# Two transformer layers on one core: heads' outputs with v as the weight, combine weights made in the small experts' loop, queries and values from split operands

## The reference

```python
h = layernorm(tok_w[x] + pos_w + type_w[mask]) * gamma + beta            # (32, 128, 192)
xn = layernorm(h)
h += softmax(causal(xn @ Wq @ Wk.T @ xn.T)) @ (xn @ Wv)                  # one head of 192
x = layernorm(h); logits = x @ phi_n.T                                   # 1024 slots = 64 experts x 16
slots = softmax(logits, over tokens).T @ x                               # dispatch
ys = gelu(layernorm(slots) @ w1[n] + b1[n]) @ w2[n] + b2[n]              # 64 small experts, hidden 384
h += softmax(logits, over slots) @ ys                                    # combine
q, k, v = split(layernorm(h) @ w_qkv.T); q, k = rope(q), rope(k)         # 12 heads of 16
h += softmax(q @ k.T) @ v @ w_proj.T + b_proj                            # no mask
x = layernorm(h); e = argmax(softmax(x @ router_w))                      # 8 experts, 512 rows each
h += gate * gelu(gelu(x @ w1[e] + b1[e]) @ w2[e] + b2[e])                # hidden 768
```

## Time and profile before

| what | value |
|---|---|
| time, median of 3 runs | 1556.29 us (1554.89 to 1559.04) |
| the profiled execution | 1558.22 us, its span 1556.5 us |
| tower, until PE's last slot sums | to about 382 us |
| small experts | to about 929 us |
| combine | to about 1402 us |
| large experts | to the end |
| busy share of the span | PE 92%, PEld 82%, DVE 63%, ACT 57%, POOL 17% |
| mean granted clock of TensorE | 0.934 |

### The profile page before, as it was taken

The page is one execution under the profiler, slowest core; times in us unless marked ns, Lnnn a source line. Parts: engine busy times, 40 slices in busy tenths (PEclk is TensorE's granted clock), DMA queues, the critical chain, the costliest instruction groups (busy, mean ns, idle before and its releaser), DMA issues. The chain is left out here.

```text
span 1556.5 us, 28510 instructions
## 1 busy us (share of the span) xinstructions
PE 1431.4 (92%) x8824; PEld 1269.1 (82%) x8824; DVE 978.6 (63%) x2877; ACT 891.0 (57%) x1833; POOL 270.8 (17%) x255
## 2 busy tenths in 40 slices
PE   3899999985899999999999986999999999957995
PEld 1577777774799999999999976999999999956985
DVE  6776666442777777777777744777776777632231
ACT  1377777774666666666666642655555555524551
POOL 5411100000111111111111101122121212120434
PEclk9999999998899999999999997889898989867998
DMA  7035655576466666666666654434333436105542
GB/s 198 25 123 146 146 135 135 140 172 149 136 200 186 193 189 196 187 190 197 189 189 190 199 155 148 129 108 126 114 125 99 121 116 190 31 11 148 134 91 20
DMA packets 202698, 220.87 MB, mean 142 GB/s; under 512 B 30065, under 2 KB 169528, under 8 KB 202606
## 3 DMA queue, kind: packets, MB, share of 16 engines
q1 hardware_dynamic: 170254, 179.96, 41.5%
q10 hardware_dynamic: 24672, 32.79, 6.2%
q0 software_dynamic: 7680, 6.95, 2.4%
HBM read 142.27 MB, written 79.90 MB: 143 GB/s over the span
## 5 line engine op out<-in xcount | busy, mean ns | idle before, releaser
L1062 PE MATMUL bank<-e_w,e_h_full 128*128 128x192 f32 x1920 | 324.5, 326 | 0.3
L1062 PEld LDWEIGHTS bank<-e_w,e_h_full 128*128 128x128 f32 x1920 | 310.6, 190 | 1.2 <-ACT e_h_full L1123 0.8
L1123 ACT ACTIVATE e_h_full<-bank,e_b 128x512 f32<-128x512 f32 x240 | 165.1, 689 | 196.7 <-PE bank L60 196.7
L1000 POOL TENSOR_TENSOR e_ln_rstd<-e_ln_var_eps,minus_half 128x4 f32<-128x4 f32 x64 | 64.8, 1013 | 524.2 <-DVE e_ln_var_eps L1173 524.2
L1180 DVE TENSOR_SCALAR e_rows<-e_slot_sums,e_ln_mean_var,e_ln_rstd 128x192 f32<-128x192 f32 x256 | 79.9, 376 | 76.2 <-POOL e_ln_rstd L1000 76.2
L1096 ACT ACTIVATE e_x_full<-bank,e_ln_shift,e_ln_gain 128x512 f32<-128x512 f32 x128 | 92.6, 773 | 53.3 <-PE bank L1035 48.5
L585 DVE TENSOR_REDUCE column_neg_max<-bank 128x4 f32<-128x512 f32 x64 | 44.3, 692 | 115.1 <-PE bank L60 103.7
L1351 POOL TENSOR_TENSOR ln_rstd<-ln_var_eps,minus_half 128x2 f32<-128x2 f32 (+1 forms) x35 | 51.8, 1481 | 345.5 <-DVE ln_var_eps L1652 345.5
L60 PE MATMUL bank<-e_x_hi,e_w1hi 128*128 128x512 f32 x240 | 105.4, 439 | 5.3 <-DVE e_w1lo L1159 3.5
L830 PE MATMUL bank<-x,dispatch_weights 128*128 128x193 f32 x512 | 97.0, 333 | 14.1 <-ACT slot_stage L690 13.5
L1412 PE MATMUL bank<-slot_out_and_one,combineT 128*128 128x193 f32 x512 | 94.5, 338 | 10.9 <-DMA slot_out_and_one<-slot_outputs 10.9
(11 more groups left out here) (214 smaller groups left out, 3071.5 us busy)
## 6 DMA issues: line engine op xcount, KB each, us to landing
slot_sums<-slot_stage SPq DMA_DIRECT2D x64, 386.0 KB
e_slot_sums<-slot_sums SPq DMA_DIRECT2D x64, 386.0 KB, 3.6
slot_outputs<-e_stage ACTq DMA_DIRECT2D x64, 384.0 KB, 3.4
slot_out_and_one<-slot_outputs SPq DMA_DIRECT2D x32, 768.0 KB
e_w<-in_w SPq DMA_DIRECT2D x64, 288.0 KB, 3.0
slot_logits<-kept_logits SPq DMA_DIRECT2D x64, 256.0 KB
slot_logits<-slot_logits SPq DMA_DIRECT2D x32, 512.0 KB, 3.4
e_w1raw<-in_w SPq DMA_DIRECT2D x80, 192.0 KB, 2.7
```

Source lines behind the costliest of these rows:

```text
L1000: pool.tensor_tensor(rs[u][:], ve[u][:], half[:], ALU.pow).then_inc(rstd_ready, 1)
L1062: last = pe.matmul(ybank(u)[:, j // 2, (j % 2) * D:(j % 2 + 1) * D], hf[:, k, js], w2s[u][:, k, :], start=k == 0, stop=k == MT - 1)
L1123: act.activation(hf[:, m, :], hbank(u, m), act_fn, bias=b1s[:, m, ds(n, 1)]).then_inc(acted, 1)
```

## The change

**Tower.** `queries` and `values` become split products: x, M and Wv have a high part (ACT) and a low part (DVE), five fp32r matmuls of 128 rows take the place of four plain fp32 instructions; the 64 odd rows are repeated so that all operands have 128. Both queries now stand in slot 1, both evictions in slot 2.

**Small experts.** A new class `Weigher` makes the combine weights here, one batch in each turn of two experts: SP loads the batch's logits and maxima, DVE adds them (`less_max`, end of u = 0), ACT takes the exponential (`exp`, end of u = 1) and stores 512 KB (`store`, end of u = 0 of the next turn). There is one buffer `weigh_out`. Before the last phase's `scalar` ACT waits for all stores.

**Combine.** The ready weights are loaded straight into `combineT`, two buffers; L1505 and L1567 are gone. The head outputs have v, padded to 32 columns, as weight and `pT` as the moving operand, each head into 32 partitions of the result, four heads side by side; the sums come from the exponentials (`accum_out`), their inverse is spread over 384 columns (DVE), transposed (PE, 3), copied (ACT) and multiplied in (DVE). The projection has three blocks of 128 rows instead of 128 + 65, the two transposes of `attn_out` and their copies are gone. The combine product stands first in PE's turn. Router and counts move 128 columns instead of 8 and 16. The two layernorms of a turn have a rsqrt each on POOL.

```diff
+    def load(self, sp, b):
+        past(sp, self.less, b)
+        sp.dma_start(self.lg[:], self.T["lg"][ds(b, 1), :, :, :].rearrange("a p c t -> p (a c) t")).then_inc(self.lg_in, 16)
+        sp.dma_start(self.nmb[:], self.T["nm_rows"][ds(b, 1), :].rearrange("a t -> (a t)").partition_broadcast(P)
+                     ).then_inc(self.lg_in, 16)
+
+    def less_max(self, dve, b):
+        dve.wait_ge(self.lg_in, 32 * b + 32)
+
+        past(dve, self.stored, 16 * b)
+        dve.tensor_tensor(self.cw[:], self.lg[:], self.nmb[:].unsqueeze(1).broadcast_to([P, NC, P]), ALU.add
+                          ).then_inc(self.less, 1)
+
+    def exp(self, act, b):
+        act.wait_ge(self.less, b + 1)
+        act.activation(self.cw[:], self.cw[:], ACT.Exp).then_inc(self.exped, 1)
+
+    def store(self, act, b):
+        act.wait_ge(self.exped, b + 1)
+        act.dma_start(self.T["cw"][ds(b, 1), :, :, :].rearrange("a p c t -> p (a c) t"), self.cw[:]).then_inc(self.stored, 16)
...
-            sp.wait_ge(self.T["kept_stored"][u], 16 * ((NG * NC + 2 - u) // 3))
...
                 def attn(a, s):
+                    if s == 0:
+                        dve.wait_ge(xT_hi_ready, a + 1)
+
+                        past(dve, v_done, 2 * a)
+                        dve.tensor_tensor(xTlo[:], xT[:, 0, :], xThi[:, 0, :].bitcast(F32), ALU.subtract)
+                        dve.scalar_tensor_tensor(xTboth[:], xThi[:, 1, :].bitcast(F32), T["minus_upper"][:, 0:1],
+                                                 xT[:, 1, :], ALU.mult, ALU.add).then_inc(xT_split, 1)
...
-                    matmuls(pe, b[0:c.stop - c.start], [(T["M0"][:, c], xT0[:]), (T["M1"][:, c], xT1[:])]
-                            ).then_inc(q_done, 1)
+                    matmuls(pe, b[0:c.stop - c.start], [
+                        (Mhi[:, 0, c], xThi[:, 0, :]), (Mlo[:, 0, c], xThi[:, 0, :]), (Mhi[:, 0, c], xTlo[:]),
+                        (Mhi[:, 1, c], xTboth[:]), (Mlo[:, 1, c], xTboth[:])]).then_inc(q_done, 1)
...
-                        last = matmuls(pe, pair((b4, b7)[k])[:, j, :], [(xT0[:, js], T["Wv0"][:]),
-                                                                       (xT1[:, js], T["Wv1"][:])])
+                        last = matmuls(pe, pair((b4, b7)[k])[:, j, :], [
+                            (xThi[:, 0, js], Wvhi[:, 0, :]), (xThi[:, 0, js], Wvlo[:, 0, :]), (xTlo[:, js], Wvhi[:, 0, :]),
+                            (xTboth[:, js], Wvhi[:, 1, :]), (xTboth[:, js], Wvlo[:, 1, :])])
...
-                    if a is not None and s < 2:
-                        queries(a, s)
+                    if a is not None and s == 1:
+                        queries(a, 0)
+                        queries(a, 1)
...
+                    if weigh is not None and (not isinstance(i, int) or i + 1 < turns):
+                        weigh.load(sp, i + 1)
...
+                        if weigh is not None and u == 1:
+                            weigh.exp(act, i)
+                        if weigh is not None and u == 0 and (not isinstance(i, int) or i > 0):
+                            weigh.store(act, i - 1)
...
                 send(n_exp - 1, 1)
+                if weigh is not None:
+                    weigh.store(act, turns - 1)
...
                                           ALU.add).then_inc(y_added, 1)
+                        if weigh is not None and u == 0:
...
+                    if y is not None:
+                        if y == 0:
+                            pe.wait_ge(S["ones_set"], 4)
+                        pe.wait_ge(ys_in[u], 16 * (y // 2 + 1))
+                        pe.wait_ge(cT_in[u], 16 * (y // 2 + 1))
+
+                        past(pe, S["h2_ready"], y)
+                        past(pe, S["x4_split"], y)
+                        for c in range(NC):
+                            last = pe.matmul(bank[:, 0, 0:D + 1], cT[u][:, c, :], ysb[u][:, c, :],
+                                             start=c == 0, stop=c == NC - 1)
+                        last.then_inc(S["Y_done"], 1)
                     if q is not None:
...
+                        past(pe, S["v_took"], q)
                         for o_, c, done in ((bank[:, 2, 0:2 * D], slice(0, 2 * D), "qk_done"),
                                             (bank[:, 3, 0:D], slice(2 * D, 3 * D), "v_done")):
...
-                            pe.wait_ge(tables_in, 64)
-                        pe.wait_ge(S["oT_took"], 2 * p + 2)
...
-                        past(pe, S["h2_ready"], y)
-                        past(pe, S["x4_split"], y)
-                        for c in range(NC):
-                            last = pe.matmul(bank[:, 0, 0:D + 1], cT[:, c, :], ysb[u][:, c, :],
-                                             start=c == 0, stop=c == NC - 1)
-                        last.then_inc(S["Y_done"], 1)
+                            pe.wait_ge(tables_in, 48)
+                        pe.wait_ge(S["o_ready"], p + 1)
+                        matmuls(pe, projected, [(oT[:, g * P:(g + 1) * P], Wp[:, g, :]) for g in range(3)]
+                                ).then_inc(S["p_done"], 1)
                     if r is not None:
                         bank7_free(pe, a, r, z)
                         pe.wait_ge(S["x5_ready"], 2 * r + 2)
...
                     if a is not None:
-                        pe.wait_ge(S["o_ready"], a + 1)
-
-                        past(pe, S["h3_ready"], a)
-                        pe.transpose(bank[:, 1, 0:P], o[:, 0:P], ident[:])
-                        pe.transpose(bank[0:DR, 1, P:2 * P], o[:, P:D], ident[:]).then_inc(S["oT_done"], 1)
+                        past(pe, S["qk_took"], min(t, NB))
+                        pe.wait_ge(S["einv_ready"], a + 1)
+                        for g in range(3):
+                            last = pe.transpose(bank[:, 2, g * P:(g + 1) * P],
+                                                einv_wide[:, g, :, :].rearrange("p s d -> p (s d)"), ident[:])
+                        last.then_inc(S["einvT_done"], 1)
+                        pe.wait_ge(S["pT_took"], 3 * a + 3)
+                        pe.wait_ge(S["v_took"], a + 1)
+
+                        past(pe, S["h3_ready"], t - 2)
+                        for g in range(3):
+                            for s in range(4):
+                                last = pe.matmul(bank[32 * s:32 * s + 32, 1, g * P:(g + 1) * P], vs[u][:, 4 * g + s, :],
+                                                 pT[:, s, g, :], start=True, stop=True)
+                        last.then_inc(S["head_out_done"], 1)
 
                 each_turn(turn)
 
             @block.scalar
...
+                                                      bias=nmx[:, s, g:g + 1], accum_out=esum[:, s, g:g + 1])
                             last.then_inc(S["S_exp"], 1)
                     if q is not None:
                         if q == 0:
...
-                        for s in range(4):
-                            dve.wait_ge(S["S_done"], 4 * a + s + 1)
-                            dve.tensor_reduce(nmx[:, s, :], group4(bank[:, 4 + s, :])[:, 0:3], AX_X, ALU.max,
+                        for k in range(2):
+                            dve.wait_ge(S["S_done"], 4 * a + 2 * k + 2)
+                            dve.tensor_reduce(nmx[:, 2 * k:2 * k + 2, :], bank[:, 4 + 2 * k:6 + 2 * k, 0:3 * P]
+                                              .rearrange("p s (g n) -> p s g n", g=3), AX_X, ALU.max,
                                               negate=True).then_inc(S["head_max"], 1)
+                    if p is not None:
+
+                        dve.wait_ge(S["head_out_done"], p + 1)
+                        past(dve, S["p_done"], p)
+                        dve.wait_ge(S["einvT_took"], p + 1)
+                        dve.tensor_tensor(oT[:], head_out, einvT[:], ALU.mult).then_inc(S["o_ready"], 1)
...
+                    if a is not None:
+                        dve.wait_ge(S["S_exp"], 4 * a + 4)
+                        past(dve, S["einvT_done"], a)
+                        st.link(dve.reciprocal(einv[:], esum[:]))
+                        dve.tensor_copy(einv_wide[:], einv[:].rearrange("p s g -> p g s").unsqueeze(3)
+                                        .broadcast_to([P, 3, 4, 2 * HD])).then_inc(S["einv_ready"], 1)
```

More of the change, by code:

```diff
@@ L210, in load_first_weights, with __init__, wait_logits @@
             self.load_w2(sp, u, u)
+class Weigher:
+    def __init__(self, sb_of, sem_of, T):
+        self.T = T
+        self.lg, self.nmb = sb_of.sb("weigh_logits", [P, NC, P]), sb_of.sb("weigh_neg_max_rows", [P, P])
+        self.cw = sb_of.sb("weigh_out", [P, NC, P])
+        self.lg_in, self.less, self.exped = sem_of.sem("weigh_logits_in"), sem_of.sem("weigh_less_max"), sem_of.sem("weigh_exp")
+        T["cw_stored"] = self.stored = sem_of.sem("weigh_stored")
+    def wait_logits(self, sp):
+        for u in range(3):
+            sp.wait_ge(self.T["kept_stored"][u], 16 * ((NG * NC + 2 - u) // 3))
+        sp.wait_ge(self.T["nm_stored"], 16 * NG)
```

(6 more changed lines are left out.)

315 lines of the change are left out of this document (152 added, 163 removed).

## The result

The changed kernel takes 1609.54 us (median of 4 runs, 1604.70 to 1615.64), the kernel before 1557.64 beside it: a ratio of 1.034, 95% interval 1.030 to 1.038. The profiled execution has a span of 1603.0 us against 1556.5. Where the 46.5 us went shows in four times of each profile: the starts of the first and last output addition of the small experts and of the large ones (`e_stage`, `e_ysum`).

The account below looks back on a forecast made before the run. PE was taken to bound the small experts (full clock) and combine (0.85). Tower -20, small experts +94 and clock +26, seam +3, combine -51 gave +52 on 1558.2: forecast 1610 us, range 1556 to 1662.

Parts of the forecast that it names:

- closed cycle through the store: Small experts: less_max waits for the previous batch's store; 15.6 us plus landing 3.9 makes a turn 19.5, +94 in 31.
- one of my signs: Small experts: DVE's less_max would be seen waiting for the DMA of weigh_out; no size given for the wait.
- the floor: Small experts, without the store: ACT's chain of 5.13 us from e_x_hi to the GELU costs +2.33 per turn, +72.
- R4: Small experts: clock falls in every turn, or the landing is 5.5; +26 to +50 more, 1636 to 1660; chance 0.12.
- R5: Small experts: each table load holds ACT 1.28 us longer than its row, 79 us more, 1687; chance 0.02.
- R3: Combine head outputs: column groups run one after another, so combine gains some 15 us instead of 51, 1645; chance 0.12.
- half of 1.5: Combine: clock partly recovers as some narrow work goes, -0.75 us per turn; the ends were 0 and -1.5.
- The limit of 11.2: Combine: DVE's work and waits keep a turn from falling below 11.2 us, so the gain ends at 62.
- The seam: After the small experts: the last store (3.9 us) must land before the next phase's scalar work, +3 us.
- R1: Small experts: table loads cost nothing on the path and the store lands early; total -61, 1495 to 1505; chance 0.11.
- R2: Experts lose only +72, no clock loss, combine gains 62: total -7, 1549; chance 0.05.
- The turning point: Whole kernel: tower, seam and combine sum to -68, so 68 us lost in the small experts cancels the gain.

Follow-up runs that it names:

- exp_early: The changed kernel with the exponential of a turn ahead of take_x instead of behind it, both table loads kept: 1577.87 us, 1.017 to the kernel before.
- store_early: The changed kernel with the store of a batch's weights right behind its exponential: 1658.49 us, 1.059 to the kernel before.
- copy_for_exp: The changed kernel with a copy for the exponential in the small experts, the exponential taken in place in combine: 1492.56 us, 0.961 to the kernel before.
- pause_filled: The changed kernel with nine more matmuls, result unread, in PE's pause before the third chunk: 1566.99 us, 1.003 to the kernel before.
- weights_in_combine: The changed kernel's tower and combine parts, with logits and maxima added and exponentiated in combine, not among the small experts: 1516.62 us, 0.978 to the kernel before.

## Why the prediction was right, step by step

The forecast of 1610 and the range held, and so did the case: tables alternate, PE waits at the third chunk. Part of the closeness is luck: four terms were off, and they cancel.

- **The experts' pause.** The place, the releaser and the two loads were as told. Mis-sized was which chain holds the turn. I took the closed cycle through the store, 15.6 plus a landing of 3.9, for a turn of 19.5. The landing is 2.6, so the cycle is 18.2, and the addition hardly waits, against one of my signs. What holds is what I had put down as the floor: a chain of 5.13 us from the end of `e_x_hi`, 2.33 too long. Measured from start to start it is 2.33, and with the pause filled a turn is 18.91, 16.48 + 2.33 + 0.1. exp_early shortened this chain and store_early lengthened it (49 us more by the medians), and the time followed both, with the clock's part in each. The term was 94 and should have been 72. The closed cycle is real all the same: in copy_for_exp, where the loads are gone, it shows as the next limit.
- **The clock.** I charged 1.7 us in half of the turns; it falls behind 28 of 31 waits, 1.6 to 1.7 us each (the two kinds of turns of exp_early, and pause_filled), some 46 us instead of 26. This was R4 in part. The two errors cancel: 120 forecast, 119.4 measured (72 + 46 = 118).
- **The table loads.** copy_for_exp puts them, with the clock's fall that they bring, at 105 of the 119 us. Each is 1.28 us in the trace, as before. "ScalarE: Activation LUTs", a page of the Trainium skill, prices a switch at 2.66 us in its section "What ACT_TABLE_LOAD costs", with a drain beside the load. The trace disagrees here: the exponential starts at 648.15, 0.01 after its load ends, and the GELU 0.01 after its own, and each load starts 0.02 after the activation ahead of it ends. R5 was wrong. The page's advice to batch work by table set, in its section "Table sets: the hidden batching unit", is what the runs bear out.
- **Combine.** -2.08 per turn, 64 us in 31, where I had -1.65 and 51. The heads gave 1.81 from start to start, the 1.8 that I had; the column groups ran side by side, and R3 was wrong. The clock came back whole, and I gave half of 1.5: that is the term that was off. Against it stand waits of 0.7 us per turn (PE is busy 290.1 of 310 us), near the 0.5 taken. With these the terms add to some -2.2; 0.1 stays unplaced. The limit of 11.2 that I put on a turn by DVE is close to the measured 11.11; weights_in_combine shows that the turn does stand on DVE's order. The seam and the stage's ends cost 5.7 us instead of 3.
- **The tower.** -13.9 in the changed kernel and 12 by itself, for -20. What failed is that nothing new waits after the second group: PE waits 15 us more for ACT's eviction chain.
- **R1 and R2** fell with the pause. The turning point, 68 us of loss in the experts, fits pause_filled: 74.8 lost there, 72.7 gained elsewhere, and a ratio of 1.003. Without the table loads the same change is 4% faster than before.

## What to carry to other kernels

Before a second activation function goes into a loop, count the loads per pass and follow them to the next activation that PE needs: it is the chain from the last free point to there that is paid, not ACT's busy share, which was 0.62 before and 0.69 after. A pause of 2 us on PE costs its own length and, here, in most turns three quarters of that again through the clock, so that filling it with useless work helps. When one limit is taken away, look for the next in the same rows: without the loads the store's cycle held the turn. Test a large change by its parts: tower and combine were worth 2% together with the maxima added in combine and 5% without them, and the third part hid it.

## What was not expected of the hardware

- At a pause of 1.75 to 1.79 us once per turn the clock fell in some turns and held in others (exp_early: turns of 18.5 and 20.2 us); at 2.17 it fell in 28 turns in a row (0.56 over 3.8 us in the row above), and yet it had held behind a pause of 3.17 just before the first of them (428.25); with nine matmuls in it, it stayed at 1.00. So the length of the pause alone doesn't decide it, and no run shows what does.
- A DMA issued on ACT right behind the activation whose output it stores keeps ACT from the next activation for 1.0 us (652.13, the exponential's end, to 653.16), and its landing took a median of 6.4 us instead of 2.6. The landing is no constant of the transfer: the same 512 KB, issued at the same place as in the changed kernel, took 4.6 us in copy_for_exp.
